# Pacing the gathers and scatters of a routed feed-forward stage by their number instead of by a look-ahead of eight tiles

## The reference, cut to what matters

```
logits = -dist2 + x @ rw.T + rb
topv, topi = top_k(logits, 4)
w = softmax(topv)
hidden = gelu(x @ w1[e].T + b1[e])         # 128 -> 512, for each chosen expert e
exp_out = hidden @ w2[e].T + b2[e]         # 512 -> 128
fused = sum(w * exp_out over the 4 chosen)
x = x + layernorm(fused)
```

## Time and profile before

| | |
|---|---|
| device time, median of 3 runs | 698.85 us (696.63 to 700.03) |
| span of the profiled execution | 694.4 us |
| median less that span | 4.45 us |
| mean granted PE clock, as a share of full speed | 0.923 |
| busy over the span | PE 536.4, DVE 364.9, ACT 353.7, POOL 281.1 us |
| gathers, scatters | 128 of 980 ns mean, 128 of 1002 ns mean |
| first `up` of step 0, first of step 157 | 237.9 us, 659.9 us |

### The profile page before, as it was taken

The page is one execution under the profiler, slowest core; times in us unless marked ns, Lnnn a source line. Parts: engine busy times, 40 slices in busy tenths (PEclk is TensorE's granted clock), DMA queues, the critical chain, the costliest instruction groups (busy, mean ns, idle before and its releaser), DMA issues.

```text
span 694.4 us, 19926 instructions
## 1 busy us (share of the span) xinstructions
PE 536.4 (77%) x6242; PEld 481.6 (69%) x6242; DVE 364.9 (53%) x1325; ACT 353.7 (51%) x1079; POOL 281.1 (40%) x308
## 2 busy tenths in 40 slices
PE   4999879994502789977678789789977776679984
PEld 4967779993401489976677679678967776668942
DVE  6554779997999356545434553112334432233126
ACT  6524167775556365546445667336634434335513
POOL 4000000000451543566666743664566666645520
PEclk9999999998655799999999999999999989989998
DMA  8970000006001455444444645445866644546553
GB/s 229 255 280 9 3 3 0 0 0 243 1 1 76 120 161 157 138 131 131 131 140 143 204 124 162 135 144 146 264 207 180 183 130 133 145 122 192 174 197 122
DMA packets 55746, 92.28 MB, mean 133 GB/s; under 512 B 10352, under 2 KB 26096, under 8 KB 55152
## 3 DMA queue, kind: packets, MB, share of 16 engines
q1 hardware_dynamic: 45424, 72.35, 35.0%
q0 software_dynamic: 10240, 18.89, 9.2%
HBM read 78.07 MB, written 17.37 MB: 137 GB/s over the span
## 4 chain that ended last, share of the span: by engine, by line
PE 43%; issue 18%; DVE 18%; POOL 8%; ACT 7%; DMA 2%; DVEq 2%; another core or an unknown queue 0%; POOLq 0%; SPq 0%; ACTq 0%
PE bank L2148 15%; PE bank L2141 13%; POOL yd L600 6%; ACT value L883 3%; DVE shared L1187 2%; DVE shared L1179 2%; POOL shared L592 2%; DVE early L1467 2%; PE bank L1735 2%; DMA shared<-yd 1%; PE bank L1772 1%; PE bank L1840 1%; PE bank L1762 1%; PE bank L2133 1%; PE bank L2089 1%
## 5 line engine op out<-in xcount | busy, mean ns | idle before, releaser
L883 ACT ACTIVATE value<-bank,shared 128x128 f32<-128x128 f32 x632 | 180.8, 376 | 203.0 <-PE bank L2141 156.7
L2148 PE MATMUL bank<-shared,value 128*128 x1264 | 182.7, 290 | 62.4 <-ACT value L883 41.7
L2148 PEld LDWEIGHTS bank<-shared,value 128*128 128x128 f32 x1264 | 161.7, 200 | 76.7 <-issue 76.1
L2141 PE MATMUL bank<-early,shared 128*128 x1264 | 180.9, 288 | 5.3 <-issue 2.8
L592 POOL DMA_INDIRECT shared<-xd,early x128 | 125.5, 980 | 127.5 <-PE bank L2141 79.8
L2141 PEld LDWEIGHTS bank<-early,shared 128*128 128x128 f32 x1264 | 162.6, 200 | 9.3 <-issue 8.4
L1663 DVE SCALAR_TENSOR_TENSOR early<-bank,value,early 128x128 f32 x158 | 55.4, 351 | 195.8 <-PE bank L2148 116.6
L600 POOL DMA_INDIRECT yd<-early x128 | 128.3, 1002 | 67.8 <-DVE early L1663 36.2
L560 POOL TENSOR_TENSOR shared<-shared,xn 128x512 f32<-128x512 f32 x4 | 5.1, 1264 | 174.9 <-DVE xn L1262 167.1
L2133 PE MATMUL bank<-ident,shared 128*128 128x128 f32 x128 | 35.9, 284 | 9.0 <-DMA shared<-xd,early 5.7
L2003 PE MATMUL bank<-ksp,shared 128*128 128x32 bf16 x1536 | 40.9, 177 | 0.0
(11 more groups left out here) (334 smaller groups left out, 689.3 us busy)
## 6 DMA issues: line engine op xcount, KB each, us to landing
shared<-w1b SPq DMA_DIRECT2D x158, 258.0 KB
w1b<-in_w_t SPq DMA_DIRECT2D x1, 4096.0 KB, 17.8
shared<-col_dram SPq DMA_DIRECT2D x1, 4096.0 KB, 13.4
shared<-in_w_t SPq DMA_DIRECT2D x1, 4096.0 KB, 12.3
att<-yd SPq DMA_DIRECT2D x8, 512.0 KB
shared<-yd SPq DMA_DIRECT2D x4, 1024.0 KB, 9.1
xd<-xnT SPq DMA_DIRECT2D x2, 1280.0 KB
shared<-xd,early POOLq DMA_INDIRECT x128
```

What stands on the lines that cost most here:

```text
L883: ins = act.activation(hT[:, i % 2, tok(c)], bank[2 + i % 2][:, tok(c)], ACT.Gelu, bias=w1_now[:, i % WR, F + c:F + c + 1])
L2141: ins = mm(bank[2 + i % 2][:, tok(c)], w1_now[:, i % WR, tok(c)], x_now, start=True, stop=True)
L2148: ins = mm(bank[6 + i % 2][:, 0:D], hT[:, i % 2, tok(c)], w2_sb[:, bass.ds(e, 1), c, :] .rearrange("p a d -> p (a d)"), start=(c == 0), st ...
```

## The change

It takes away the look-ahead limit of the gathers (NEAR) and puts one counter over gathers and scatters. Move number k of the queue (k = 0 to 255) waits until `up_ps` has reached (k - HEAD) * 158 / 256, rounded down, with HEAD = 4; at zero or less it does not wait. All other waits stay. BEHIND goes from 27 to 34, so that in each half 34 gathers stand ahead of the first scatter, and 34 scatters after the last gather of the second half.

```diff
-    BEHIND = 27
+    BEHIND = 34
...
-    NEAR = 8
+    HEAD = 4
...
+            moved = [0]
+
+            def in_step():
+                freed(pool, up_ps, (moved[0] - HEAD) * IALL // (2 * JALL))
+                moved[0] += 1
+
             def rows(n):
-                if n >= NEAR:
-                    pool.wait_ge(up_ps, step_of(n) - NEAR + 1)
+                in_step()
...
             def results(m):
+                in_step()
                 pool.wait_ge(y_ready, step_of(m) + E)
```

## The result

| | before | changed |
|---|---|---|
| median of the runs | 699.44 us (696.63 to 700.08, 4 runs) | 674.97 us (671.26 to 676.09, 4 runs) |
| ratio, 95% interval | | 0.9652 (0.9611 to 0.9693) |
| span of the profiled execution | 694.4 us | 673.8 us |
| first `up` of step 0 | 237.87 us | 244.84 us |
| the 158 steps | 423.04 us | 395.12 us |

The change makes the kernel 3.5% faster. In the profiled executions the 158 steps became 27.9 us shorter, the stage began 7.0 us later, and the tail is the same: -27.9 + 7.0 + 0.35 = -20.6 us of span. The medians lie 24.5 us apart, 4 us more than these spans: the profiled execution of the kernel before (696.63 us) was the fastest of its four, that of the changed kernel (675.91) one of its slower ones.

The account below looks back on a forecast made before the run. POOL's moves, with PE's signals late behind unbroken runs, were taken to bound the crowded steps. At 2.60 us a step, -36.8 us there and smaller terms elsewhere sum to -19.7: 698.85 becomes 679 us, range 648 to 708.

Parts of the forecast that it names:

- In these stretches the stage thus goes at the pace of POOL's moves: Steps 20 to 57 and 99 to 136, a gather and a scatter each: 1.52 us a move, 234.4 us.
- PE's signals come about 1 us after POOL has stopped: While moves follow without rest, signals reach ACT and POOL late; gelu 1.03 us, next gather 1.26 us after POOL stops.
- The step of 1.62 moves at 2.60 us: Evenly spread moves, 256 / 158 a step: 2.60 us taken, nearer to (a) and (b) than to (c).
- (a): Signals still come in pairs of steps: blocks of 3.24 moves take 5.11 us, 2.55 us a step.
- (b): Each step its own block: two-move steps cost 3.04 us, one-move steps 2.06, giving 2.67 us a step.
- (c): Moves cost 1.52 us each as now, giving 2.46 us a step.
- Steps 72 to 85: Rest of 6.79 us before gather 64 stays; shorter PE waits for gathers and POOL's pace give -4.0 us.
- It fits: Scatters 34 behind with 32 result slots: two steps, 5.2 us, cover a move and a landing, 0.98 + 3.27.
- The clock: Quiet stretches would lose full clock, 0.94 in place of 1.00 over 73 us, costing 2 us.
- Twice the gain, short blocks set free: Rival, chance 0.14: blocks of at most two moves are covered, step 2.2 to 2.3 us, -61 us, 638 us.
- No gain: Rival, slower case, chance 0.19: delay belongs to the pair of steps, 6.1 us with three moves; 719 to 734 us.
- The edit does nothing: then POOL is full: POOL always later than its level: 252 x 1.28 = 323 us, faster than forecast; given no separate chance.

Follow-up runs that it names:

- the first ten experiments: All follow-up runs except the one without scatters and the one with added copies; kernel before took 642.8, 643.5 and 645.3 us on their three chips.
- the second profile: The changed kernel run again unaltered, beside the kernel before on another chip: 613.90 us, ratio 0.9503.
- the second group: Changed kernel again (0.9503), kernel before again (1.0003), and the changed kernel without the `up_ps` wait, 27 behind (0.9765) or with BEHIND_2 = 11 (0.9462).
- the run without scatters: Kernel before with its 128 result tiles sent by SP in plain transfers to fixed rows, not scattered by POOL: 619.20 us, ratio 0.8852.

## Why the prediction was right, and where it was off

It said 679 us (648 to 708) and faster with 0.74; measured were 674.97. The forecast of the crowded steps was right on the traces it was made from; that these were traces with late signals, which most of the experiments don't have, it could not know.

- **"In these stretches the stage thus goes at the pace of POOL's moves"**: right, and more widely than I had it: POOL's moves and rests add up to the whole stage. In the quiet stretches of the kernel before, though, it is POOL that waits for PE.
- **"Nor is POOL simply full"**: half right. In the first traces POOL rested 16.1 and 23.0 us in the crowded stretches, so the rests were real. But on the one faster chip with a trace of the kernel before it is full there, with no rest at all, and two moves at 1.29 us are longer than PE's step. I took the rests for the cause; they stood on top of a queue that was full in any case. I had written the floor (1.28 us a move) and used it only as a bound.
- **PE's signals come about 1 us after POOL has stopped**: true of the first result's chip, before and after, and false on the three chips of the first ten experiments. The pattern was read rightly, but belongs to the chip or the time it was read at and not to the kernel; its cause stays open.
- **The step of 1.62 moves at 2.60 us, by blocks of 3.24 moves (a)**: measured 2.55 and 2.53 in the crowded stretches; (a) said 2.55, with a rest of 1.26 where blocks of three rest 1.19.
- **The sum**, -19.7 us against -27.9 measured:

| steps | predicted | measured |
|---|---|---|
| 20 to 57 and 99 to 136 | -36.8 | -41.3 |
| 86 to 98 | +7.1 | +5.0 |
| 0 to 19 | +5.5 | +4.9 |
| 58 to 71 | +1.4 | -1.2 |
| 72 to 85 | -4.0 | +0.1 |
| 137 to 157 | +7.1 | +4.5 |

  The mechanism was right and the mis-sized term is the step, 2.60 for 2.53 to 2.55 in the crowded stretches, 2.45 over steps 86 to 98, and less than I took in steps 58 to 71 and 137 to 157 too. Steps 72 to 85 are off the other way. The sum was 8.2 us short, and the 7.0 us by which the profiled execution began later hide most of it: the span of 675 us that I forecast met one of 673.8 by luck. The median then lies 1.2 us above that span and not the 4.45 that I had kept, because the profiled execution of the kernel before was its fastest.
- **Two slips in the working.** By its own list 137 steps are put at 2.60 us (76, 13, 20, 10, 7 and 11), not 120; (a), (b) and (c) would then move the sum by 7, 10 and 19 us in place of 6, 8 and 17. And moves number 4 and 5 have a level of zero, so 250 moves got the wait and not 252. Neither changes the range.
- **Steps 72 to 85** won nothing. PE's wait for gathers did shrink, to 0.6 us:

```profile
L2139 PE MATMUL bank<-ident,shared 128*128 128x128 f32 x128 | 35.0, 278 | 0.6 <-DMA shared<-xd,early 0.6
```

  But after the rest before gather 64 POOL made eight moves in one run, 421.22 to 431.2 us, the gelu of step 72 was 7.40 us late, and steps 72 and 73 took 5.13 and 6.48 us. On the faster chip the same kernel has no such delay, and the same steps take 30.5 us in place of 42.0.
- **"It fits"** of the result slots: shown by its opposite. In the changed kernel this line of DVE (1658 there) waits for no scatter in the first result and 2.4 us in the second profile; under the old limit the same 34 cost 41.7 us of it.
- **The clock.** I gave 2 us for the rule of the Trainium skill (TensorE: Matmul & The Clock Gate, section "HAM oscillation — how this bites in real kernels") in the quiet stretches. The sum was wrong: a mean of 0.94 over 73 us costs up to 0.06 x 73 = 4.4 us, not half of that. The reading was narrow too, since the earlier trace rows also have 1.00 over steps 72 to 78, where PE is busy 72%, and 0.95 where it is busy 92%. In the changed kernel the granted clock rose from 0.96 and 0.92 to 1.00 in the crowded stretches, where PE is busy 88 and 83% of the time, and stayed at 1.00 over steps 86 to 98 at 89%. It fell a little over steps 0 to 19 (1.00 to 0.97) and 137 to 157 (0.97 to 0.96), and far over steps 72 to 78, to 0.78, where the two long steps lie. In step 72 PE had stood 2.79 us for a gelu, and step 73 ran at the lower of the two levels, 1.2 GHz:

```profile
428.24 1.39 PE L2154 MATMUL bank<-shared,value 128*128 x8 [2.79 <-ACT value L889]
...
429.42:435.90 6.48, 3.99 (x18) 3.60 (x18) 0.70 (x2) 2.50 (x10) 3.73 (x5) 0.50 0.39 109
```

  So the rows bear the rule out in that one place; in the other stretches the even spread cost next to nothing of the clock.
- **The rivals.** "Twice the gain, short blocks set free" would have needed the gelu within 0.1 us of `up` in most steps. On the first chip that did not come (it is so in 29 of the changed kernel's 158 steps); on the chip of the second group it is so in over 150 steps of both kernels, and the change still brings only 29.3 us, since POOL's queue, and behind it PE's own work, are the limits there with prompt signals too. "No gain" had its place in two steps with three moves taking 6.1 us; they took about 4.7 (585.57 to 590.37 is 4.80, with one move of 1.22).
- **"The edit does nothing: then POOL is full"** I set aside as no separate case. On the faster chips it is nearly the case: taking the wait out altogether gives 0.947 beside 0.950.

What stays open: why PE's signals come late in some sets of runs while POOL's moves follow each other. In the run without scatters, where all moves but 12 stand alone, the lateness is gone on such a chip; that does not tell whether the scatters or the unbroken runs bring it. No limit with 34 behind was not run on a chip of that kind, where its runs of moves could cost what they win elsewhere; on the others it can't be told from the changed kernel, so no version here is shown to beat it.

## What to carry to other kernels

Where one in-order queue serves two kinds of work, compare its moves times the cost of one with the length of each stretch. If the queue is full in half of the stretches and partly idle in the others, time is won back by letting it work ahead. The distance between the kinds, the limit on working ahead and the number of slots have to be changed together. Test the parts of such a change one by one before dropping one: here they are 1.034 and 0.992 alone and 0.950 together. What can be won ends where the next engine is full, here PE. And before a delay is built into a model, see whether another chip shows it.

## What the runs showed of the hardware that was not expected

- The same kernel takes 642.8, 643.5 and 645.3 us on three chips, and 699.4 and 699.8 us in the two other sets of runs. The two profiles of it (638.6 and 694.4 us of span) differ by 56.4 us in the 158 steps and by less than 1 us elsewhere. In the slower one the gelu begins 1.12 us after `up` in the mean, in the faster one 0.05; the mean granted clock was 0.923 and 0.933. Whether the chip or the time of the run makes the difference, and why, is not shown.
- An indirect transfer of 128 rows keeps POOL for 0.97 to 0.99 us in the mean of each run plus 0.306 us to the next one, on every chip and however long the run (137 in a row, 1.29 us apart). A memset of 0.327 us with its wait between them adds 0.305 us from start to start, not 0.327: it begins as the transfer ends, and 0.28 us follow it.
